# Token selection of a vision tower: score sum and mean from one narrow product on the uncentred tokens, variance from the transposed tokens

## The reference, cut to what matters

```python
t = tokens.transpose(0, 2, 3, 1).reshape(b, n, d)
mu = jnp.mean(t, axis=-1, keepdims=True)
var = jnp.mean(jnp.square(t - mu), axis=-1, keepdims=True)
ln = (t - mu) * jax.lax.rsqrt(var + LN_EPS) * norm_w + norm_b
scores = jnp.einsum('bnd,d->bn', ln, fc_w[0]) + fc_b[0]
scores = jax.nn.softmax(scores, axis=-1)
_, idx = jax.lax.top_k(scores, num_keep)
idx = jnp.sort(idx, axis=-1)
selected = jnp.take_along_axis(t, idx[:, :, None], axis=1)
```

## Time and profile before

| | |
|---|---|
| time before, median of 3 runs | 4198.61 us (4191.21 to 4204.34) |
| profiled execution: its time, its span | 4186.22 us, 4184.4 us |
| TensorE busy, share of the span | 3328.6 us, 80% |
| VectorE busy, share of the span | 2690.6 us, 64% |
| ScalarE busy, share of the span | 2261.0 us, 54% |
| GpSimd busy, share of the span | 702.1 us, 17% |
| granted TensorE clock over the span | 0.865 of full speed |

### The profile page before, as it was taken

The page is one execution under the profiler, slowest core; times in us unless marked ns, Lnnn a source line. Parts: engine busy times, 40 slices in busy tenths (PEclk is TensorE's granted clock), DMA queues, the critical chain, the costliest instruction groups (busy, mean ns, idle before and its releaser), DMA issues. The chain is left out here.

```text
span 4184.4 us, 61280 instructions
## 1 busy us (share of the span) xinstructions
PE 3328.6 (80%) x22648; PEld 1688.7 (40%) x22649; DVE 2690.6 (64%) x4527; ACT 2261.0 (54%) x4791; POOL 702.1 (17%) x696
## 2 busy tenths in 40 slices
PE   7549999999999999964878888749995997544385
PEld 6224333444334343333443434323334775333253
DVE  1528889888888889956777777424442333246386
ACT  1138989898889889952556555613332331211143
POOL 1220111111111111120000000024430001102654
PEclk7559999999999999986999998969997798766698
DMA  2041001111010010021000000143323122440112
GB/s 46 1 110 28 21 21 29 31 34 36 21 31 21 21 31 21 21 53 44 9 8 9 10 8 10 36 106 73 78 55 99 35 47 46 122 94 23 31 33 60
DMA packets 114675, 168.46 MB, mean 40 GB/s; under 512 B 67635, under 2 KB 92596, under 8 KB 106444
## 3 DMA queue, kind: packets, MB, share of 16 engines
q1 hardware_dynamic: 99764, 153.24, 16.2%
q0 software_dynamic: 5248, 5.71, 0.5%
q10 hardware_dynamic: 9393, 5.88, 0.5%
HBM read 86.55 MB, written 40.19 MB: 30 GB/s over the span
## 5 line engine op out<-in xcount | busy, mean ns | idle before, releaser
L1003 DVE TENSOR_REDUCE att_NM<-att_ring 121x1 f32<-121x1024 f32 x1088 | 1259.1, 1214 | 187.1 <-PE att_ring L850 185.9
L924 ACT ACTIVATE att_ring<-att_ring,att_NM 121x1024 f32<-121x1024 f32 x1088 | 1184.3, 1089 | 176.4 <-DVE att_NM L1003 170.7
L848 PE MATMUL att_ring<-att_q,att_k 64*121 64x512 f32 x2176 | 1182.9, 652 | 58.0 <-ACT att_ring L924 29.3
L850 PE MATMUL att_ring<-att_q,att_k 64*121 64x512 f32 x2176 | 1183.0, 652 | 0.0
L848 PEld LDWEIGHTS att_ring<-att_q,att_k 64*121 64x121 f32 x2176 | 354.1, 189 | 750.1 <-ACT att_ring L924 529.4
L1377 ACT ACTIVATE gqa_PT<-gqa_ring 121x484 f32<-121x484 f32 (+3 forms) x912 | 359.4, 450 | 199.6 <-PE gqa_ring L1304 132.6
L1421 DVE TENSOR_REDUCE gqa_NM<-gqa_ring 121x1 f32<-121x484 f32 (+1 forms) x720 | 375.0, 578 | 120.6 <-PE gqa_ring L1281 80.1
L850 PEld LDWEIGHTS att_ring<-att_q,att_k 64*121 64x121 f32 x2176 | 354.2, 189 | 0.0
L1304 PE MATMUL gqa_ring<-gqa_QS,gqa_KS 128*121 128x484 bf16 (+3 forms) x912 | 271.3, 328 | 35.9 <-ACT gqa_PT L1377 23.1
L1281 PE MATMUL gqa_ring<-gqa_KS,gqa_QS 128*121 128x484 bf16 (+1 forms) x720 | 253.5, 377 | 41.2 <-ACT gqa_PT L1377 19.1
L1761 DVE TENSOR_TENSOR moe_hh<-moe_sg,moe_p 128x484 f32<-128x484 f32 x204 | 134.3, 658 | 201.4 <-ACT moe_sg L1698 201.4
(11 more groups left out here) (444 smaller groups left out, 5140.4 us busy)
## 6 DMA issues: line engine op xcount, KB each, us to landing
moe_xw<-route_weights SPq DMA_DIRECT2D x17, 968.0 KB, 7.2
att_k<-att_k SPq DMA_DIRECT2D x32, 512.2 KB, 6.4
att_q<-att_q SPq DMA_DIRECT2D x32, 512.2 KB, 8.3
n_T<-h SPq DMA_DIRECT2D x40, 192.0 KB, 4.1
by_freq<-stu_Yf SPq DMA_DIRECT2D x32, 160.0 KB
stu_YT<-by_freq SPq DMA_DIRECT2D x8, 640.0 KB, 5.6
moe_fs<-x_moe SPq DMA_DIRECT2D x4, 1028.5 KB, 10.4
sel_X<-in_x SPq DMA_DIRECT2D x4, 1024.0 KB
```

The costliest lines, as they stand in the source:

```text
L848: nc.tensor.matmul(to[0:TT, 0:512], lo[0:64, par, TT * t:TT * t + TT], mlo[0:64, par, CK * ck:CK * ck + 512], start=True, stop=True)
L850: nc.tensor.matmul(to[0:TT, 512:1024], hi[64:128, par, TT * t:TT * t + TT], mhi[64:128, par, CK * ck + 512:CK * ck + 1024], start=True, st ...
L924: nc.scalar.activation(to[0:TT, :], to[0:TT, :], ACT.Exp, bias=NM[0:TT, turn % 2, g, ck:ck + 1], accum_out=SS[0:TT, turn % 2, g, ck:ck + 1 ...
L1003: nc.vector.tensor_reduce(NM[0:TT, turn % 2, g, ck:ck + 1], slot("score", turn, n)[0:TT, :], AX.X, ALU.max, negate=True).then_inc(S["max_r ...
```

## The change

The sixteen `MEAN64` products and GpSimd's squares go. A product of `MEAN64` with the one column of weights (`vec[:, 4:5]`, new L196) gives the mean of the weights, which VectorE takes off them; with weights that sum to zero, the weighted sum over the uncentred tokens is that over the centred ones. `G` now has four columns: two of these weights, two of 1/64. One product of `X` with the four columns (new L207) gives sum and mean of each token in `pU`. It stands behind the four transposes of the same 512 tokens (new L204), which now go round four banks of PSUM. VectorE subtracts the mean, read from `pU` and spread over 64 channels, from `XT` (new L302); ScalarE squares (new L260); VectorE adds the squares up (new L305). The weighted sums are then multiplied by the inverse root in two halves (new L314, L315).

```diff
-        pDot = r.ps("pDot", [128, 4, NB])
-        pVar = r.ps("pVar", [128, 4, NB])
+        pU = r.ps("pU", [128, 2, 512])
-        pMean = [pA, pB]
+        pTurn = [pT[:, 0, :], pT[:, 1, :], pA[:, :], pB[:, :]]
...
+        per_token = lambda t, g, k: t[:, g, 4 * k:4 * k + 4, :].rearrange("p i (h d) -> p i h d", h=2)
+        stats = lambda g: pU[:, g, 0:4 * NB].rearrange("p (i x) -> p i x", x=4)
...
-                for k in range(NCH):
-                    if k >= 2:
-                        pe.wait_ge(centred, k - 1)
-                    nc.tensor.matmul(pMean[k % 2][:, :], const(MEAN64), flat(X)[:, 512 * k:512 * k + 512],
-                                     start=True, stop=True).then_inc(mean_ready, 1)
-                for k in range(NCH):
-                    if k >= 2:
-                        pe.wait_ge(turned_out, k - 1)
-                    for j in range(4):
-                        ins = nc.tensor.transpose(pT[:, k % 2, 128 * j:128 * j + 128],
-                                                  flat(X)[:, 512 * k + 128 * j:512 * k + 128 * j + 128], const(EYE))
-                    ins.then_inc(turned, 1)
-                pe.wait_ge(centred, NCH)
-                pe.wait_ge(squared, NCH)
+                pe.wait_ge(weight_ready, 1)
+                nc.tensor.matmul(pM[:, 4:5], const(MEAN64), vec[:, 4:5], start=True, stop=True).then_inc(weight_mean, 1)
                 pe.wait_ge(g_ready, 1)
                 for g in range(2):
-                    for i in range(NB):
-                        nc.tensor.matmul(pDot[:, g:g + 3:2, i], XC[:, g, 128 * i:128 * i + 128], G[:, :],
-                                         start=True, stop=True)
-                        ins = nc.tensor.matmul(pVar[:, g:g + 3:2, i], SQ[:, g, 128 * i:128 * i + 128],
-                                               C[:, 128:256:64], start=True, stop=True)
+                    for k in range(NG):
+                        n = NG * g + k
+                        if n >= 4:
+                            pe.wait_ge(turned_out, n - 3)
+                        for j in range(4):
+                            ins = nc.tensor.transpose(pTurn[n % 4][:, 128 * j:128 * j + 128], flat(X)[:, 512 * n + 128 * j:512 * n + 128 * j + 128], const(EYE))
+                        ins.then_inc(turned, 1)
+                        for j in range(4):
+                            ins = nc.tensor.matmul(stats(g)[:, 4 * k + j, :], flat(X)[:, 512 * n + 128 * j:512 * n + 128 * j + 128], G[:, :],
+                                                   start=True, stop=True)
+                    ins.then_inc(stats_ready, 1)
...
-                for k in range(NCH):
-                    pool.wait_ge(centred, k + 1)
-                    c = slice(512 * k, 512 * k + 512)
-                    nc.gpsimd.tensor_tensor(flat(SQ)[:, c], flat(XC)[:, c], flat(XC)[:, c], ALU.mult).then_inc(squared, 1)
...
+                for n in range(NG):
+                    turn_out(n)
+                for k in range(NG):
+                    turn_out(NG + k)
+                    square(0, k)
+                for k in range(NG):
+                    square(1, k)
...
-                for k in range(NCH):
-                    c = slice(512 * k, 512 * k + 512)
-                    dve.wait_ge(mean_ready, k + 1)
-                    nc.vector.tensor_tensor(flat(XC)[:, c], flat(X)[:, c], pMean[k % 2][:, :], ALU.subtract).then_inc(centred, 1)
+                for g in range(2):
+                    dve.wait_ge(stats_ready, g + 1)
+                    for k in range(NG):
+                        dve.wait_ge(turned_out, NG * g + k + 1)
+                        mean = stats(g)[:, 4 * k:4 * k + 4, 2:4].rearrange("p i (h a) -> p i h a", a=1).to_broadcast((128, 4, 2, 64))
+                        nc.vector.tensor_tensor(per_token(XC, g, k), per_token(XT, g, k), mean, ALU.subtract).then_inc(centred, 1)
+                    for k in range(NG):
+                        dve.wait_ge(squared, NG * g + k + 1)
+                        nc.vector.tensor_reduce(VR[:, g:g + 3:2, 4 * k:4 * k + 4].rearrange("p h i -> p i h"), per_token(SQ, g, k), AX.X, ALU.add).then_inc(summed, 1)
                 dve.wait_ge(dots_ready, 1)
+                dve.wait_ge(summed, NCH)
```

More of the change, by code:

```diff
@@ L79, in stage_select @@
         X = r.sb("X", [128, 2, NTOK])
-        XC = r.sb("XC", [128, 2, NTOK])
-        SQ = r.sb("SQ", [128, 2, NTOK])
         XT = r.sb("XT", [128, 2, NB, 128])
+        XC = r.sb("XC", [128, 2, NB, 128])
+        SQ = r.sb("SQ", [128, 2, NB, 128])
+        VR = r.sb("VR", [128, 4, NB])
         HS = r.sb("HS", [128, 2 * N + 128])
@@ L85, in stage_select @@
         vec = r.sb("vec", [128, 8])
-        G = r.sb("G", [128, 2])
+        G = r.sb("G", [128, 4])
         S = r.sb("S", [128, 128])
@@ L114, in stage_select @@
         pT = r.ps("pT", [128, 2, 512])
-        pDot = r.ps("pDot", [128, 4, NB])
-        pVar = r.ps("pVar", [128, 4, NB])
+        pU = r.ps("pU", [128, 2, 512])
         pM = r.ps("pM", [128, 512])
-        pMean = [pA, pB]
+        pTurn = [pT[:, 0, :], pT[:, 1, :], pA[:, :], pB[:, :]]
         loaded = r.sem("loaded")
-        mean_ready = r.sem("mean_ready")
+        weight_ready = r.sem("weight_ready")
+        weight_mean = r.sem("weight_mean")
+        stats_ready = r.sem("stats_ready")
+        summed = r.sem("summed")
         centred = r.sem("centred")
@@ L158, in stage_select @@
         NCH = 2 * NTOK // 512
+        NG = NCH // 2
         flat = lambda t: t[:, :, :].rearrange("p g n -> p (g n)")
+        per_token = lambda t, g, k: t[:, g, 4 * k:4 * k + 4, :].rearrange("p i (h d) -> p i h d", h=2)
+        stats = lambda g: pU[:, g, 0:4 * NB].rearrange("p (i x) -> p i x", x=4)
         NLOAD = 16 * (4 + 1 + 10)
@@ L257, in _, with turn_out, square @@
             def _(act):
-                xt = XT[:, :, :, :].rearrange("p g i n -> p (g i n)")
-                for k in range(NCH):
-                    act.wait_ge(turned, k + 1)
-                    nc.scalar.copy(xt[:, 512 * k:512 * k + 512], pT[:, k % 2, :]).then_inc(turned_out, 1)
+                def turn_out(n):
+                    act.wait_ge(turned, n + 1)
+                    nc.scalar.copy(XT[:, n // NG, 4 * (n % NG):4 * (n % NG) + 4, :].rearrange("p i n -> p (i n)"), pTurn[n % 4]).then_inc(turned_out, 1)
+                def square(g, k):
+                    act.wait_ge(centred, NG * g + k + 1)
+                    nc.scalar.activation(SQ[:, g, 4 * k:4 * k + 4, :], XC[:, g, 4 * k:4 * k + 4, :], ACT.Square).then_inc(squared, 1)
+                for n in range(NG):
[5 more added lines that the diff above has]
+                    square(1, k)
                 act.wait_ge(var_ready, 1)
@@ L280, in _ @@
                 dve.wait_ge(loaded, NLOAD)
-                ch(nc.vector.tensor_tensor(vec[:, 4:5], vec[:, 0:1], vec[:, 2:3], ALU.mult))
-                ch(nc.vector.tensor_scalar(G[:, :], C[:, 128:256:64], vec[:, 4:5], 64.0, ALU.mult, ALU.mult))
+                nc.vector.tensor_tensor(vec[:, 4:5], vec[:, 0:1], vec[:, 2:3], ALU.mult).then_inc(weight_ready, 1)
+                dve.wait_ge(weight_mean, 1)
+                ch(nc.vector.tensor_tensor(vec[:, 5:6], vec[:, 4:5], pM[:, 4:5], ALU.subtract))
+                ch(nc.vector.tensor_scalar(G[:, 0:2], C[:, 128:256:64], vec[:, 5:6], 64.0, ALU.mult, ALU.mult))
+                ch(nc.vector.tensor_copy(G[:, 2:4], C[:, 128:256:64]))
                 ch(nc.vector.scalar_tensor_tensor(out=col[:, 0:1], in0=vec[:, 1:2], scalar=0.5, in1=vec[:, 2:3],
@@ L286, in _ @@
                 nc.vector.memset(ZR[:, :], 0.0).then_inc(g_ready, 1)
-                for k in range(NCH):
-                    c = slice(512 * k, 512 * k + 512)
-                    dve.wait_ge(mean_ready, k + 1)
-                    nc.vector.tensor_tensor(flat(XC)[:, c], flat(X)[:, c], pMean[k % 2][:, :], ALU.subtract).then_inc(centred, 1)
+                for g in range(2):
[7 more added lines that the diff above has]
+                        nc.vector.tensor_reduce(VR[:, g:g + 3:2, 4 * k:4 * k + 4].rearrange("p h i -> p i h"), per_token(SQ, g, k), AX.X, ALU.add).then_inc(summed, 1)
                 dve.wait_ge(dots_ready, 1)
-                nc.vector.tensor_scalar(S[:, :], pVar[:, :, :].rearrange("p b i -> p (b i)"), LN_EPS, None, ALU.add).then_inc(var_ready, 1)
+                dve.wait_ge(summed, NCH)
+                nc.vector.tensor_scalar(S[:, :], VR[:, :, :].rearrange("p b i -> p (b i)"), 1.0 / 64, LN_EPS, ALU.mult, ALU.add).then_inc(var_ready, 1)
                 ch(nc.vector.tensor_tensor(vec[:, 7:8], pM[:, 0:1], vec[:, 3:4], ALU.add))
@@ L296, in _ @@
                 ch(nc.vector.reciprocal(P[:, :], RS[:, :]))
-                ch(nc.vector.tensor_tensor(J[:, :], P[:, :], pDot[:, :, :].rearrange("p b i -> p (b i)"), ALU.mult))
+                in_g = lambda t, g: t[:, :].rearrange("p (b i) -> p b i", b=4)[:, g:g + 3:2, :]
```

(2 more changed lines are left out.)

## The result

The changed kernel takes 4172.63 us (median of 8 runs, 4157.15 to 4179.18), the kernel before 4200.21 us (8 runs, 4188.89 to 4204.89). The ratio is 0.9935, 95% interval 0.9918 to 0.9952: faster by 27.6 us. The forecast was 4174 us. The profiled execution has a span of 4155.3 us.

A forecast was written before the change was run, and what follows sets the result against it. Bound: the serial path through TensorE's 128 narrow products at half clock to the ranking. 105.71 - 80.8 - 0.2 = 24.7 us gained, off the 4198.6 median gives 4173.9; range 4154 to 4186 for 8 in 10.

The forecast's parts named there:

- Half clock throughout: TensorE's new stretch of transposes and narrow products stays at 1.2 GHz, narrow products 0.43 us apart; chance 78%.
- signs of being wrong: Clock at 1.00 between 30 and 70, gaps between L204 and L207, L302 or L305 much over 0.7 us, later stage growing.
- The case with the rising clock: Rival: the clock rises in TensorE's alternating stretch, 21.5 us instead of 41.3, gain 44.5, time 4154; chance 9%.
- Step 1: Before TensorE's stretch: transposes wait for VectorE's centred weights and start at 28.80 us, a delay of 2.0 us.
- Step 2: TensorE's stretch: 16 turns of 2.58 us, 41.3 us, transposes at 0.22; second `stats_ready` at 70.5 us.
- Step 3: VectorE's tail: second group starts at 70.7 us, sixteen bare instructions take 10.0 us, ranking begins at 80.8.
- Step 4: Behind the ranking's start: two half multiplications instead of L297 lose 0.2 us.
- bubbles: Rival: 32 changes between transposes and products on TensorE each expose a 0.21 us load, 6.8 us; time 4181; chance 5%.
- the tail's instructions: Rivals: VectorE's sixteen take twice as long, 12 us more (no measurable change, 4186, 5%), or 37.3 us more (slower, 4211, 3%).
- loss behind the barrier: Rival: later stages give the gain back, so no measurable change, 4186 us; chance 5%, shared with a tail 12 us longer.

The follow-up runs named there:

- run 4: The changed kernel with the moving operand of its 64 narrow products widened from 4 to 128 columns; 4159.83 us, ratio 0.9902 to the kernel before.
- Run 5: The changed kernel with VectorE centring each 512 tokens once their four products are out, adding the previous turn's squares; 4164.52 us, ratio 0.9913 to the kernel before.
- run 2: The changed kernel with constants loaded first, 22 wide products during image loading and two more behind L196; ranking started at 74.55 us, against 78.17.
- run 6: The changed kernel with transpose and narrow product merged into one 132-column product, three blocks a turn, VectorE turn by turn; 4141.17 us, ratio 0.9868 to the kernel before.

## Why the prediction was right

The gain was forecast as 24.7 us and measured as 27.5 in the trace, 27.6 between medians; 2.8 us off, all of it in terms that I had costed too dear: 2.2 by the start of the second group, 0.4 in the tail, 0.2 behind it. That the time came within 1.4 us of 4174 is in part luck, since the median of the kernel before was 1.6 us higher in this comparison than the one I had started from.

- **Half clock throughout**: right, by the durations, and the choice on which the size hung. One of my signs of being wrong came up even so, a clock that reads 1.00 between 30 and 70. The sign was badly chosen: the earlier trace rows had shown that the column reads 1.00 in this stage at the durations of half clock. The case with the rising clock needed something wide: run 4 made it happen by columns alone. The Trainium skill, "TensorE: Matmul & The Clock Gate", "Why this matters for your kernels", has the rule that I had weighed: keep TensorE busy and it reaches full clock. It is not borne out: 39.3 us without a gap stayed at half.
- **Step 1**: TensorE begins at 28.75 (28.80 forecast; the loads ended 0.1 us earlier).
- **Step 2**: the stretch took 39.3 us (28.75 to 68.02), not 41.3. The term that was mis-sized is the transpose: a turn took 2.45 us, of which the narrow products are 8 x 0.213 = 1.71, which leaves 0.19 for a transpose and not the 0.22 that I had from doubling its step at full clock. The bound from above, 0.27, was farther off still.
- **Step 3**: the mechanism held. The second group waited for the last sum of the first, and that for ScalarE's eighth square (67.85); it started at 68.45 (70.7 forecast, 2.0 of the difference by the shorter stretch). Sixteen instructions took 9.7 us (10.0 forecast, 9.7 the lower bound): the steps are 0.60, as where no instruction waits for its neighbour. The spread operand cost nothing, 0.68 us against the 0.69 of the earlier trace rows. Run 5 took the tail away and got its price.
- **Step 4**: nothing was lost to the end of the multiplications. The two half multiplications cost 0.07 us, and the first instruction, which now reads SBUF, is 0.06 shorter: 78.17 to 80.22, as from 105.71 to 107.76. The 0.7 us that was lost behind them, ahead of the barrier, I had not in the sum.
- **The rivals**: no bubbles between transposes and products (turn 2.45 without gaps); the tail's instructions were not dear; no loss behind the barrier shows above what those stages vary by. The rising clock I had priced right by the turn (1.34; 1.33 in run 4) and too high in all: in run 4 the first two turns took 2.61 and 1.95 us, before the clock had risen and while it rose, and the stretch took 23.2 us, not 21.5.

## What to carry to other kernels

A product with few moving columns costs the loads of its stationary block, so count blocks loaded and not columns computed. Columns up to the width of the load were nearly free here (128 in place of 4 cost 0.05 us in a turn of 1.28 at full clock, run 4 against run 2). And they are worth more than nothing: on work that narrow products would leave at 1.2 GHz, more columns past the same loads brought 2.4 GHz (run 4), and merging the narrow product with the transpose of the same block brought both fewer loads and the full clock (run 6). When one engine hands over by groups, look at what remains of the next engine's work behind the last group (run 5).

## What the runs showed of the hardware

- The level of TensorE's clock followed what it streamed and not how busy it was. Busy without a gap at 0.50: 26.4 us of the mixture with four columns (run 2). At 1.00: 19.5 us of the same order with 128 (run 4, 178 instructions at 0.11 us each, which bears the column out).
- With 22 wide products ahead of it, the clock read 0.50 behind the idle stretch of run 2 (24.9 to 27.9).
- The stages behind vary too, by about half of what this change gives. The attention stage's 1088 activations as a group of the changed kernel (first and last start stand as A to B):

```profile
L942 ACT ACTIVATE att_ring<-att_ring,att_NM x1088: 1073/1090/1104, 290.2 to 1787.7; 121x1024 f32<-121x1024 f32 x182
```

The same group in the kernel of run 5:

```profile
L953 ACT ACTIVATE att_ring<-att_ring,att_NM x1088: 1072/1088/1103, 283.5 to 1795.8; 121x1024 f32<-121x1024 f32 x182
```

1497.5 us in the one, 1512.3 in the other, on the same code, one trace of each kernel. One profiled span thus can't rank versions 10 us apart; the start of the ranking can, and medians over several runs roughly can. What makes that stage vary stays open.
